# Sixteen-head attention on one core: row loads in pieces of four heads, first q stores on ScalarE's queue, table load behind the rounding

## The reference

```
logits = q_h @ k_h.T / sqrt(8) + mask
probs = softmax(logits)
out_h = probs @ v_h
```

## Time and profile before

| | |
|---|---|
| median of 3 runs | 1611.69 us (1608.59 to 1616.65) |
| the profiled execution | 1612.87 us, span 1611.0 us |
| mean granted TensorE clock | 0.882 |
| busy: PE, DVE, ACT, POOL | 76%, 61%, 55%, 34% |
| row loads of the three plain stages | 24 of 384 KB, median 5.6 us to landing |
| row loads of L3_attn | 8 of 384 KB, median 6.2 us to landing |

### The profile page before, as it was taken

One profiled execution on the slowest core, in us unless ns is written; L12 is line 12 of the kernel. 1 busy time (PEld: TensorE's weight loads), 2 busy tenths in 40 slices (PEclk: granted clock), 3 DMA queues, 4 the chain that ended last, 5 costly groups with the idle time before them and its releaser, 6 DMA issues. The chain is left out here.

```text
span 1611.0 us, 21115 instructions
## 1 busy us (share of the span) xinstructions
PE 1222.6 (76%) x6990; PEld 612.9 (38%) x6990; DVE 982.2 (61%) x1994; ACT 880.8 (55%) x1817; POOL 541.6 (34%) x673
## 2 busy tenths in 40 slices
PE   8999637366666668976757977958867988979886
PEld 3675412022222224532223543433443433733462
DVE  3673465999999836612956635436435748727752
ACT  3673244699999745864025861244623755723653
POOL 1462014588888823200313211001101213603440
PEclk9999887599999987997987997976886999999998
DMA  3000000000000036001025100024114310000000
GB/s 147 1 2 3 20 9 0 0 0 1 0 0 1 0 103 127 2 34 40 0 85 128 32 18 1 0 50 95 26 54 100 60 54 1 2 1 1 1 2 13
DMA packets 43340, 48.75 MB, mean 30 GB/s; under 512 B 3040, under 2 KB 40032, under 8 KB 42080
## 3 DMA queue, kind: packets, MB, share of 16 engines
q1 hardware_dynamic: 43232, 47.40, 11.2%
HBM read 34.28 MB, written 13.11 MB: 29 GB/s over the span
## 5 line engine op out<-in xcount | busy, mean ns | idle before, releaser
L1524 POOL TENSOR_TENSOR L_attn_z<-L_attn_state,L_attn_r 128x1024 f32<-128x1024 f32 x64 | 150.9, 2359 | 21.5 <-DVE L_attn_state L1510 14.6
L1510 DVE TENSOR_TENSOR_SCAN L_attn_state<-bank,L_attn_w 128x512 f32<-128x512 f32 x128 | 148.9, 1205 | 0.0
L1421 PE MATMUL bank<-L_attn_z,const 128*128 128x512 f32 x256 | 139.7, 674 | 0.2 <-POOL L_attn_z L1528 0.2
L926 DVE CUSTOM_DVE_ANT_0 L_xattn_core_logits<-bank,L_xattn_mask 128x256 f32<-128x256 f32 x256 | 98.6, 422 | 54.2 <-PE bank L707 41.6
L1461 ACT ACTIVATE L_attn_r<-L_attn_after_dt,L_attn_half_guard,L_attn_A 128x512 f32<-128x512 f32 x128 | 96.5, 802 | 0.0
L1405 PE MATMUL bank<-L_attn_rows,L_attn_select 128*128 128x512 bf16 x96 | 36.0, 432 | 79.4 <-ACT L_attn_C L1473 42.7
L1451 ACT ACTIVATE bank<-L_attn_dt,L_attn_A 128x510 f32<-128x510 f32 x128 | 86.5, 676 | 12.6 <-DVE L_attn_state L1510 12.6
L838 ACT ACTIVATE L_xattn_core_probs<-bank 128x512 f32<-128x512 f32 x132 | 71.6, 596 | 37.6 <-PE bank L750 26.6
L707 PE MATMUL bank<-L_xattn_core_rows 48*128 48x256 bf16 x384 | 65.1, 314 | 31.0 <-DMA L_xattn_core_rows<-L_xattn_core_slots 16.9
L1528 POOL TENSOR_TENSOR L_attn_z<-L_attn_z,L_attn_C 128x1024 f32<-128x1024 f32 x32 | 75.7, 2366 | 23.4 <-ACT L_attn_C L1473 23.3
L1491 DVE TENSOR_TENSOR L_attn_w<-bank,L_attn_udt 128x1024 f32<-128x1024 f32 x64 | 78.2, 1221 | 5.3 <-PE bank L1405 1.6
(11 more groups left out here) (500 smaller groups left out, 3066.7 us busy)
## 6 DMA issues: line engine op xcount, KB each, us to landing
L_xattn_core_rows<-L_xattn_core_slots SPq DMA_DIRECT2D x24, 384.0 KB, 5.6
weights<-in_pack_L_ffn SPq DMA_DIRECT2D x2, 2118.5 KB, 8.2
L_xattn_core_slots<-L_xattn_core_k_parts SPq DMA_DIRECT2D x24, 128.0 KB, 2.0
L_attn_core_rows<-L_attn_core_slots SPq DMA_DIRECT2D x8, 384.0 KB, 6.2
weights<-in_pack_L_ffn SPq DMA_DIRECT2D x1, 2824.0 KB, 12.0
L_xattn_core_slots<-L_xattn_core_q_parts SPq DMA_DIRECT2D x12, 192.0 KB, 2.2
weights<-in_pack_L_xattn SPq DMA_DIRECT2D x1, 1539.5 KB, 6.8
weights<-in_pack_L_attn SPq DMA_DIRECT2D x2, 768.0 KB, 8.1
```

The source lines that it names most:

```text
L926: last = nc.vector.tensor_tensor_reduce(logits[:, c], scores_bank[side][:, c * S:(c + 1) * S], mask[:, 2 * b + c, :], 1.0, MASKED, ALU.add ...
L1421: last = nc.tensor.matmul(y_bank[2 * c + half][:], ident, z[:, g % NS, c], start=False, stop=False, skip_group_check=True)
L1510: nc.vector.tensor_tensor_scan(state[:, g % NS, c, ::step], a_bank[c][:, ::step], w[:, g % 2, c, ::step], 0.0, ALU.mult, ALU.add).then_inc ...
L1524: nc.gpsimd.tensor_tensor(z[:, g % NS], state[:, g % NS], r[:, g % NS], ALU.mult).then_inc(z_done, 1)
```

## The change

Four things change in `attention8`. The row loads of the first two batches are issued in eight pieces of 96 KB (four quads, two sides), each quad with a semaphore of its own, and TensorE waits per quad. SP no longer waits for batch 0's rows before it stores batch 1, and in the regrouped form it no longer waits for batch 2's rows before it stores batch 3. The stores of q of batch 0 are issued by ScalarE. The table set is loaded behind the rounding and, with a mask, behind ScalarE's mask work.

```diff
+    PIECEWISE = 2
...
+        quad_rows_in = [[sem(f"rows_in{b}_{j}") for j in range(NG8)] for b in range(PIECEWISE)]
...
+        def store(eng, b, n, part):
+            src = parts[n][:, part, tokens(b)]
+            for at in (SLOTS_K, SLOTS_Q)[n][part]:
+                if regrouped:
+                    for slot in range(6)[at]:
+                        eng.dma_start(slots[slot, :, :, b, n].rearrange("d h t -> h d t"), src).then_inc(stored[b], 16)
+                else:
+                    dst = slots[at, :, :, b, n].rearrange("s d h t -> (d h) s t")
+                    eng.dma_start(dst, src.unsqueeze(1).to_broadcast([P, dst.shape[1], S])).then_inc(stored[b], 16)
+        transfers = 12 if regrouped else sum(len(SLOTS_K[part]) + len(SLOTS_Q[part]) for part in range(3))
         @block.sync
         def _(sp):
             for b in range(B):
-                if b >= 1:
+                if b == PIECEWISE:
+                    for j in range(NG8):
+                        sp.wait_ge(quad_rows_in[b - 1][j], 16 * 2)
+                if b > PIECEWISE and not regrouped:
                     sp.wait_ge(rows_in[b - 1], 16 * 2)
                 for part, ready in ((0, rounded), (1, rounded2), (2, split)):
-                    for n in (KEYS, QUERIES):
+                    for n in (KEYS,) if b == 0 else (KEYS, QUERIES):
                         sp.wait_ge(ready, 2 * b + n + 1)
+                        store(sp, b, n, part)
+                sp.wait_ge(stored[b], 16 * transfers)
+                if b < PIECEWISE:
+                    for j in range(NG8):
+                        for side in range(2):
+                            sp.dma_start(rows[side_rows(side), j::NG8, b].rearrange("p h n t -> p h (n t)"),
+                                         slots[:, :, 8 * side + j:8 * side + 8:NG8, b].rearrange(
+                                             "s d h n t -> (s d) h (n t)")).then_inc(quad_rows_in[b][j], 16)
+                    continue
...
             def scores(p):
-                if p % SPB == 0:
-                    pe.wait_ge(rows_in[p // SPB], 16 * 2)
+                b, at = divmod(p, SPB)
+                if b < PIECEWISE and at % 2 == 0:
+                    pe.wait_ge(quad_rows_in[b][at // 2], 16 * 2)
+                elif at == 0:
+                    pe.wait_ge(rows_in[b], 16 * 2)
...
         @block.scalar
         def _(act):
-            nc.scalar.preload_act_table_set(LN_EXP)
             for b in range(B):
                 for i in (2 * b, 2 * b + 1):
                     nc.scalar.activation(piece(i, 0), piece(i), ACT.Copy).then_inc(rounded, 1)
+                if b == 0:
+                    act.wait_ge(rounded, QUERIES + 1)
+                    store(act, 0, QUERIES, 0)
                 for i in (2 * b, 2 * b + 1):
                     act.wait_ge(less, i + 1)
                     nc.scalar.activation(piece(i, 1), left(i), ACT.Copy).then_inc(rounded2, 1)
+                if b == 0:
+                    act.wait_ge(rounded2, QUERIES + 1)
+                    store(act, 0, QUERIES, 1)
+                    act.wait_ge(split, QUERIES + 1)
+                    store(act, 0, QUERIES, 2)
...
+            nc.scalar.preload_act_table_set(LN_EXP)
```

More of the change, by code:

```diff
@@ L659, in _ @@
             for b in range(B):
-                if b >= 1:
+                if b == PIECEWISE:
+                    for j in range(NG8):
+                        sp.wait_ge(quad_rows_in[b - 1][j], 16 * 2)
+                if b > PIECEWISE and not regrouped:
                     sp.wait_ge(rows_in[b - 1], 16 * 2)
-                count = 0
                 for part, ready in ((0, rounded), (1, rounded2), (2, split)):
-                    for n in (KEYS, QUERIES):
+                    for n in (KEYS,) if b == 0 else (KEYS, QUERIES):
                         sp.wait_ge(ready, 2 * b + n + 1)
[L666 to L678, removed]
+                        store(sp, b, n, part)
[7 more added lines that the diff above has]
+                    continue
                 for side in range(2):
```

## The result

| | median | runs | over before, 95% interval |
|---|---|---|---|
| before | 1610.9 us | 1608.59 to 1616.65, 4 runs | |
| after | 1587.8 us | 1582.52 to 1590.65, 4 runs | 0.9853 [0.9828, 0.9879] |

What follows compares the result with a forecast made beforehand. It took the starts of four stages, and SP's waits and DMA pace in L3_attn, as the bound. Gains of 3.6 + 3.8 + 5.5 + 9.5 = 22.4 us gave a median of 1589.3 us, range 1579 to 1600.

Steps and rivals of the forecast that it cites:

- The table load: Start of each stage: moved to idle ScalarE time it costs nothing, and everything at the start comes 1.28 us earlier.
- q's stores on ScalarE: Plain stages: 0.45 us per issue; last store 0.9 us earlier, 2.15 with the table; mask work 0.2 us late.
- Quads: First score: TensorE waits for a quarter of the bytes, 3.3 us instead of 6.92, so 3.6 us earlier.
- the three terms of the 3.3: Row load issue to first score: 1.7 us small-store latency, 0.4 us second issue, 1.2 us a quarter of the bytes.
- Rival (3): Row loads: first quad lands no earlier than all eight pieces; gain 15.6 us, 1596 us; chance 0.09.
- The masked stages: L1_xattn, L2_xattn: Pool's mask parts become late next, not DMA; gains 3.6 and 3.8 us.
- L3_attn: Regrouped stage: scores start 8.1 us earlier, waits at most 0.3, 4.2 and none at later batches; gain 9.5 us.
- L3_xattn: Unmasked plain stage: 2.15 us from stores and table plus 3.6 from quads, counted as a 5.5 us gain.
- just then: L3_xattn: the four warming matmuls start 1.0 us earlier and end at 1223.7, when the first score can start.
- (1): DMA issue: SP and ScalarE alternate on one descriptor generator; gain 16.2 us, 1595.5 us; chance 0.15.
- (2): Stage starts: clock may stay at 2.4 GHz and ScalarE's issues be nearly free; 6 us more, 1583; chance 0.20.
- (4): ScalarE's 15 issues take long; gain gone at 1.95 us each, 1620 us at 2.5; chance 0.02, within 0.5% 0.04.

Runs made afterwards that it cites:

- e2: Changed kernel with the table load back ahead of the rounding in each stage; 0.9905 of the kernel before.
- e1: Changed kernel with the q stores of batch 0 back on SP; 0.9901 of the kernel before.
- e5: Changed kernel with GpSimd splitting only batch 0's mask part before the first quad's shifts, the others behind the first two quads; 0.9851 of the kernel before.
- e11: e9 with q's stores of batch 0 on ScalarE in all four stages; 1583.04 us, 0.9813 of the kernel before.
- e9: Changed kernel with e5's order, q on ScalarE only in L3_attn, there quads in three batches and no row waits before stores; 1585.95 us, 0.9844 of before.
- e10: e9 with quads in L3_attn's batch 0 alone, its batches 1 to 3 loaded whole; 1585.04 us, 0.9830 of the kernel before.
- e3: Changed kernel with whole row loads in every batch, its waits kept; 0.9911 of the kernel before.
- e6: Changed kernel with two warming matmuls instead of four ahead of the first scores; 0.9874 of the kernel before.
- e7: Changed kernel with quads in three batches, batch 3's stores queued behind batch 2's quads; 0.9869 of the kernel before.

## Why the prediction was right

**The sum.** Forecast 3.6 + 3.8 + 9.5 + 5.5 (stages in the table's order) = 22.4; by the mean of three traces 3.9 + 4.6 + 9.5 + 5.0 = 23.1, and by the medians 23.1. Forecast time 1589.3, measured 1587.8. That it came so close is in part luck: in L3_attn, the largest term, two errors of about 3 us cancel, and the trace of before is a single one.

**The table load.** Right that it costs nothing in its new place (611.22, the turn four microseconds later). That everything moves 1.28 us forward was paid out in the masked stages: e2 gives 1.0 and 1.9 there. In L3_xattn it gives 0.3, and in L3_attn a change of the clock hides what the load is worth.

**q's stores on ScalarE.** Size right: taken 0.45, measured 0.34 to 0.43 in the plain form; 0.62 taken, 0.53 to 0.63 in the regrouped one. Next rounding as forecast. Row loads at 4.85, 4.80 and 4.64 us, forecast 4.34: ScalarE's last store starts at 2.65, forecast 2.55, but the rows go out 2.0 to 2.2 us behind it and not 1.7. L3_attn 6.77, forecast 6.84. What the step missed is its sign in the masked stages: the prediction said that the 1.28 us won are "eaten by the issues", and so they are, so that the step there costs an estimated 0.4 to 0.8 us net (e1, one trace) while the earlier rows it brings are idle behind Pool. When e5's order takes Pool away, the two cases come close: 100.8 and 100.2 (e5) and 100.3 and 100.5 (e11) with it, 101.9 and 100.3 (e9) and 101.1 and 100.6 (e10) without. By the whole time e1 is some 8 us slower than the changed kernel, so that taking q's stores off ScalarE in the plain stages is not shown to pay.

**Quads.** 3.3 us were forecast from issue to first score. Where TensorE waited for them, in L2_xattn and L3_attn, it was 2.7 (847.02 to 849.71) and 2.8:

```profile
847.02 3.63 SPq L687 DMA_DIRECT2D L_xattn_core_rows<-L_xattn_core_slots  x8
...
849.71 0.40 PE L722 MATMUL bank<-L_xattn_core_rows 48*128 48x256 bf16 x4 [1.13 <-DMA L_xattn_core_rows<-L_xattn_core_slots]
```

The page gives 2.3 us to landing for a load of 96 KB and 6.1 us for one of 384 KB, so the three terms of the 3.3 were half a microsecond too much together; which of them is not told apart. In the plain stages this makes up for the row loads, which go out half a microsecond late. Rival (3), first quad no earlier than the last, is excluded: in L2_xattn the first score starts 2.7 us behind the first issue, while SP needs 3.63 us for the eight.

**The masked stages.** "What is late next is Pool" is what the trace shows (2.21 us of waiting at the turn) and e5 confirms by removing it. Turn 3.3 us earlier, forecast 3.2, and the second turn follows the first in 5.37 us and not 5.79, the 0.4 us that the forecast had for the scores queued behind. L2_xattn's gain is 4.6 us and not 3.8; the rest of it comes between the second turn and the fourth, where the granted clock is back 25 us from the stage's start and not 31. That the clock gives it is likely, not shown.

**L3_attn.** Waits of 0.3 at most, 4.2 and none were forecast; 1.00, 4.07 and none stand there, and batch 2's rows go out 35.8 us from the start, forecast 35.4. (The forecast took SP's next store at 1089.02 for the first score, which stands at 1089.05; nothing hangs on it.) To batch 2's first score, 42.34 us from the start in the forecast and 42.36 in the trace, the account is right. From there two terms are wrong. The low clock behind the new wait was priced at 0.5 us; it costs 3.1, since batch 3's first score comes 18.40 us behind batch 2's and in e10, with the clock up, 15.31. An estimate from the windows agrees: of the ten microseconds from 1100 on the wait takes 1.2; at e11's 12.2 matmuls a microsecond the other 8.8 would hold 107 and hold 70, so 37 are missing, 3 us. So batch 3 starts at 60.75 us and not at the 57.84 forecast. The other term was put at nothing: the wait at batch 3 that goes away had a low clock of ten microseconds behind it as well, and without it the rest of the stage is 29.41 us and not 32.93, a gain of 3.5 us. The two cancel, and the forecast of 9.5 us is met by the mean of the three traces (10.1, 8.5 and 10.0) by luck. What the prediction did not ask is whether L3_attn would be better off without quads (e3) or with its later rows issued sooner (e9).

**L3_xattn.** 5.5 forecast, 5.0 measured. The failed step is that the warming matmuls end "just then": starting 0.8 us earlier, they had more of the lower clock in them and took 5.69 to 6.48 us, not the 5.2 of the earlier trace rows, ended last and set the first score, at 8.28 to 9.08 us from the start where the forecast has 7.8. e6 shows that this is worth nothing by itself. The half microsecond is lost later: in two of the three traces the first turn is 5.8 us early, and the fifth, which comes 5.65 us behind the fourth and not 4.94, only 5.1.

**The rivals.** (1) One descriptor resource: while ScalarE issues too, SP's six issues in L3_attn take 1.90 us for three and 1.80 for three (the 0.8 us between them is the wait for the second roundings), 0.52 to 0.63 us each; with SP alone in e1 the twelve stores take 0.58 to 0.62 us each, but for one of 0.72. ScalarE's take 1.92 and 1.83 us for three in the same microseconds. So nothing is seen of the alternation that rival (1) needs; L3_attn's rows went out as the forecast had them and e1 gives the step 3.4 us. The Trainium skill (Perfetto Trace Analysis, section on the HWDGE DMA instruction) has the descriptor block locked for exclusive use; by that rule two issues would stand one behind the other, and the runs show them side by side at their usual length, so the measurement decides against the consequence drawn from it. The Trainium skill (DMA: Bandwidth & Descriptors, section "Issuing engines are not separate DMA queues") says that issuing on several engines saves only the sequencer's time; the trace agrees, since e1's loss in L3_attn, 3.4 us, is about the six issues' 3.75 us on ScalarE. (2) A clock that stays up: not seen; in L3_xattn windows of 1 us show it down until 28 to 30 us from the start in the three traces, and before until 33. (4) Issues over 1 us on ScalarE: none.

## What to carry to other kernels

When a start is made earlier, follow the buffers and queues that feed the later batches: here the early start met batch 2's rows, and a stop of 4 us in the middle of dense matmuls cost another 3 us through the clock. Count the stops that go away the same way: the one of 2 us before had a low clock behind it that cost 3.5 us. Splitting a load into pieces pays for the batch that is waited for and delays, by its extra issues, whatever is queued behind; decide it per batch and per form. Moving DMA issues to a compute engine is paid at that engine's own next work; it showed its gain where the queue relieved was the bound.

## What the runs showed of the hardware that was not expected

- An issue on ScalarE's queue takes 0.34 to 0.63 us, no longer than on SP, and a 96 KB load of rows lands in 2.3 us (median).
- Two queues that issue at once do not slow each other: SP's head-by-head stores take 0.60 us beside ScalarE's and 0.60 alone (medians).
- A wait of 4.07 us in L3_attn, amid dense matmuls, was followed by ten microseconds at a granted clock of 0.52, 3.1 us on top of the wait. In e11, without it, the clock is 1.00 there. A wait of 2.01 us (before, batch 3) and one of 3.31 (e7, batch 3) had the same behind them, waits of 0.51 and 0.79 us at that place (e9, e11) nothing. But in e2 a wait of 3.95 us was followed by only some three microseconds of low clock.
- Two warming matmuls instead of four changed no stage by over 0.4 us.
